# Start-up of a fused S4 and gated-FFN kernel: first factors in two halves, identity on another queue, another order of folds and turns

## The reference

```
xn = layernorm(x)
s  = S4 convolution of xn along the 512 + D * xn      # a 512-tap causal filter
h1 = xn @ w1.T + 2 * (xn @ A1.T) @ B1.T               # 1376 hidden units, rank 16
h3 = xn @ w3.T + 2 * (xn @ A3.T) @ B3.T
y  = (silu(h1) * h3), through w2 with A2, B2 likewise
out = x + s * silu(y)
```

## Time and profile before

| | |
|---|---|
| median of 3 runs | 406.63 us |
| the profiled execution's own time | 406.52 us |
| its span, first to last instruction | 404.7 us |
| TensorE busy | 399.2 us (99%) |
| VectorE, ScalarE, GpSimd busy | 207.4, 111.5, 80.3 us |

### The profile page before, as it was taken

How to read it: one execution, slowest core, us unless ns; L and a number is a source line. 1 busy time by engine, 2 the same in 40 slices (tenths; PEclk the granted TensorE clock), 3 DMA queues, 4 the chain that set the end, 5 groups by cost and what they waited for, 6 DMA issues and landing times.

```text
span 404.7 us, 5106 instructions
## 1 busy us (share of the span) xinstructions
PE 399.2 (99%) x1838; PEld 332.9 (82%) x1838; DVE 207.4 (51%) x323; ACT 111.5 (28%) x185; POOL 80.3 (20%) x141
## 2 busy tenths in 40 slices
PE   8999999999999999999999999999999999999996
PEld 7988888888888888888888888888888888888885
DVE  5877776794883336553345236754236134411227
ACT  7554232222541111222232112222123111211122
POOL 6686745403510113300000101600000000000000
PEclk9999999999999999999999999999999999999999
DMA  8583743614325102000005301000002000000002
GB/s 275 147 218 97 230 149 110 209 41 126 110 89 173 52 2 52 2 1 0 2 1 193 118 0 52 0 0 0 0 0 104 2 0 0 2 0 0 2 0 104
DMA packets 14515, 26.90 MB, mean 66 GB/s; under 512 B 2816, under 2 KB 4576, under 8 KB 14368
## 3 DMA queue, kind: packets, MB, share of 16 engines
q1 hardware_dynamic: 13488, 24.53, 19.1%
q0 software_dynamic: 720, 1.60, 1.5%
q10 hardware_dynamic: 288, 0.52, 0.3%
HBM read 21.45 MB, written 4.54 MB: 64 GB/s over the span
## 4 chain that ended last, share of the span: by engine, by line
PE 95%; DVE 1%; DMA 1%; ACT 1%; issue 1%; POOL 0%; DVEq 0%; ACTq 0%; POOLq 0%
PE h L1173 19%; PE h L1175 19%; PE h L1174 19%; PE f L1173 10%; PE f L1175 10%; PE f L1174 10%; PE h L1196 2%; PE spare L1160 1%; PE spare L1175 1%; PE spare L1173 1%; PE spare L1174 1%; DMA xn<-x_dram 1%; PE spare L1155 1%; DVE xres L946 0%; ACT xn L723 0%
## 5 line engine op out<-in xcount | busy, mean ns | idle before, releaser
L1173 PE MATMUL h<-xt,w 128*128 (+2 forms) x340 | 131.3, 386 | 0.0
L1174 PE MATMUL h<-xt,w 128*128 (+2 forms) x340 | 131.2, 386 | 0.0
L1175 PE MATMUL h<-xt,w 128*128 (+2 forms) x340 | 131.1, 386 | 0.0
L913 DVE TENSOR_TENSOR ghl<-g,ghl 128x512 fp32r<-128x512 f32 x44 | 31.7, 721 | 83.5 <-ACT ghl L715 83.5
L1173 PEld LDWEIGHTS h<-xt,w 128*128 128x128 f32 x340 | 63.9, 188 | 12.8 <-DVE w L852 0.3
L1175 PEld LDWEIGHTS h<-xt,w 128*128 128x128 f32 x340 | 63.9, 188 | 12.8
L1174 PEld LDWEIGHTS h<-xt,w 128*128 128x128 f32 x340 | 63.9, 188 | 12.6
L1173 PE MATMUL f<-ghl,w2f 128*128 128x512 f32 x176 | 68.7, 390 | 0.0
L1174 PE MATMUL f<-ghl,w2f 128*128 128x512 f32 x176 | 68.6, 390 | 0.0
L1175 PE MATMUL f<-ghl,w2f 128*128 128x512 f32 x176 | 68.5, 389 | 0.0
L908 DVE TENSOR_TENSOR g<-g,h 128x512 f32<-128x512 f32 x40 | 27.5, 688 | 77.3 <-PE h L1175 77.2
(11 more groups left out here) (187 smaller groups left out, 353.0 us busy)
## 6 DMA issues: line engine op xcount, KB each, us to landing
raw<-w_dram SPq DMA_DIRECT2D x28, 256.0 KB, 4.0
outT_dram<-xres SPq DMA_DIRECT2D x15, 256.0 KB, 2.4
xres<-xT_dram SPq DMA_DIRECT2D x3, 1024.0 KB, 6.0
rows_next<-x_dram SPq DMA_DIRECT2D x4, 512.0 KB, 3.6
scale_rows<-scales_scratch SPq DMA_DIRECT2D x3, 512.0 KB, 4.1
rows<-x_dram SPq DMA_DIRECT2D x2, 512.0 KB, 6.5
dft_sb<-dft_dram SPq DMA_DIRECT2D x1, 1024.0 KB, 5.0
xres<-xT_dram SPq DMA_DIRECT2D x4, 256.0 KB, 3.9
```

Of the source, the lines that this page charges most:

```text
L913: nc.vector.tensor_tensor(ghl[:, 1, :], g[:, :], ghl[:, 0, :].bitcast(F32), ALU.subtract).then_inc(glo_done, 1)
L1173: pe.matmul(out, w[1], m[0], start=start, stop=False)
L1174: pe.matmul(out, w[0], m[1], start=False, stop=False)
L1175: return pe.matmul(out, w[0], m[0], start=False, stop=stop)
```

## The change

The first factors are stored as two halves, the first for w1, the second for w3. Each half has its own clearing (half on VectorE, half on GpSimd), its own load and semaphore. The identity and the other lane constants are issued on ScalarE's queue behind row tiles 1 and 2. The warm-up has 8 matmuls instead of 11. TensorE does turn 0, fold (1, 1), turn 1, fold (3, 1), and then the first product; the first products of w1 and w3 are taken apart into their three parts, and turns 2 and 3 stand between those. VectorE and ScalarE follow in the order of their work.

```diff
-FIRST_COLS = {1: 2 * D, 3: 2 * D + 2 * P}
+FIRST_COLS = {1: D, 3: 2 * D + 2 * P}
-FACTORS_BY_DVE = 832
+FACTORS = LORA_FIRST // 2
-A_FIRST = {1: 0, 3: D}
+A_FIRST = {1: 0, 3: D + 2 * P}
...
@@ SyncE @@
             load_tile(0)
-            sync.wait_ge(factors_dve, 1)
-            sync.wait_ge(factors_pool, 1)
-            sync.dma_start(lr[0:P:STACK_STEP, :], lora).then_inc(lora_in, 16)
-            sync.dma_start(lane_c[:, :], lanes).then_inc(const_in, 16)
+            for i in range(2):
+                sync.wait_ge(factors_dve, i + 1)
+                sync.wait_ge(factors_pool, i + 1)
+                cols = slice(i * FACTORS, (i + 1) * FACTORS)
+                sync.dma_start(lr[0:P:STACK_STEP, cols], lora[:, cols]).then_inc(lora_in[i], 16)
...
@@ ScalarE @@
             for r in (1, 2):
                 act.dma_start(xn[:, r, :], x[r * P:(r + 1) * P, :]).then_inc(x_in[r], 16)
+            act.dma_start(lane_c[:, :], lanes).then_inc(const_in, 16)
...
             rows_hi(0)
+            rows_hi(1)
             rows_norm(2)
-            rows_hi(1)
             spread_cast(spread_in, slice(0, LANES_EARLY))
+            fold_hi(3, 0)
             rows_norm(3)
-            fold_hi(3, 0)
...
@@ VectorE @@
-            nc.vector.memset(lr[:, 0:FACTORS_BY_DVE], 0.0).then_inc(factors_dve, 1)
+            for i in range(2):
+                nc.vector.memset(lr[:, i * FACTORS:i * FACTORS + FACTORS // 2], 0.0).then_inc(factors_dve, 1)
             rows_first(0)
             rows_first(1)
+            fold_add(1, 0)
             rows_first(2)
-            fold_add(1, 0)
+            fold_add(3, 0)
             rows_first(3)
-            fold_add(3, 0)
             rows_lo(0)
+            rows_lo(1)
             fold_lo(1, 0)
-            rows_lo(1)
...
@@ TensorE @@
+                def part(out, kind, w, m, cols, start, stop):
+                    for c in range(DC):
+                        mm = pe.matmul(out[:, cols], w13_tile(kind, 0, w)[:, c, :], xt[:, 0, m, c, cols],
+                                       start=(start and c == 0), stop=(stop and c == DC - 1))
+                    return mm
...
-                keep_busy(11)
-                pe.wait_ge(lora_in, 16)
+                keep_busy(8)
+                pe.wait_ge(lora_in[0], 16)
                 fold(1, 0)
+                pe.wait_ge(lora_in[1], 16)
                 fold(3, 0)
                 pe.wait_ge(const_in, 16)
                 turn_rows(0)
+                fold(1, 1)
                 turn_rows(1)
-                fold(1, 1)
-                turn_rows(2)
-
+                fold(3, 1)
                 pe.wait_ge(whi_done, 1)
                 pe.wait_ge(xhi_done, RT // 2)
-                for c in range(DC):
-                    pe.matmul(h1[:, lo], w13_tile(1, 0, 0)[:, c, :], xt[:, 0, 0, c, lo], start=(c == 0), stop=False)
-                fold(3, 1)
+                part(h1, 1, 0, 0, lo, True, False)
+                turn_rows(2)
+                pe.wait_ge(xlo_done, RT // 2)
+                part(h1, 1, 0, 1, lo, False, False)
+                wait_split(pe, 1, 0)
+                part(h1, 1, 1, 0, lo, False, True)
                 turn_rows(3)
-                wait_split(pe, 1, 0)
-                pe.wait_ge(xlo_done, RT // 2)
-                for c in range(DC):
-                    pe.matmul(h1[:, lo], w13_tile(1, 0, 1)[:, c, :], xt[:, 0, 0, c, lo], start=False, stop=False)
-                    pe.matmul(h1[:, lo], w13_tile(1, 0, 0)[:, c, :], xt[:, 0, 1, c, lo], start=False, stop=(c == DC - 1))
+                pe.wait_ge(whi_done, 2)
+                part(h3, 3, 0, 0, lo, True, False)
+                part(h3, 3, 0, 1, lo, False, False)
                 wait_split(pe, 3, 0)
-                hidden(0, 0, 0, 3, h3, lo)
+                part(h3, 3, 1, 0, lo, False, True)
+                pe.wait_ge(xhi_done, RT)
+                part(h1, 1, 0, 0, hi, True, False)
+                part(h1, 1, 1, 0, hi, False, False)
                 pe.wait_ge(xlo_done, RT)
-                hidden(0, 0, 0, 1, h1, hi).then_inc(h1_ready, 1)
+                part(h1, 1, 0, 1, hi, False, True).then_inc(h1_ready, 1)
                 hidden(0, 0, 0, 3, h3, hi).then_inc(h3_ready, 1)
...
@@ GpSimd @@
-            nc.gpsimd.memset(lr[:, FACTORS_BY_DVE:LORA_FIRST], 0.0).then_inc(factors_pool, 1)
-            pool.wait_ge(factors_pool, 1)
+            for i in range(2):
+                nc.gpsimd.memset(lr[:, i * FACTORS + FACTORS // 2:(i + 1) * FACTORS], 0.0).then_inc(factors_pool, 1)
+            pool.wait_ge(factors_pool, 2)
...
@@ host @@
-        "lora": _np.concatenate([a1, a3, b1.T[:, :2 * P], b3.T[:, :2 * P]], axis=1),
+        "lora": _np.concatenate([a1, b1.T[:, :2 * P], a3, b3.T[:, :2 * P]], axis=1),
```

More of the change, by code:

```diff
@@ L404, in build @@
         raw_in = [sem(f"raw_in{i}") for i in range(6)]
-        lora_in, const_in = sem("lora_in"), sem("const_in")
+        lora_in, const_in = [sem(f"lora_in{i}") for i in range(2)], sem("const_in")
         spread_in, late_in, stack_cleared = sem("spread_in"), sem("late_in"), sem("stack_cleared")
```

## The result

The changed kernel takes 407.79 us in the median of 12 runs (406.61 to 408.33), the kernel before, beside it, 406.73 us (406.45 to 407.12): a ratio of 1.0023, 95% interval 1.0015 to 1.0031. It is slower by 1.06 us in the medians, where 0.35 us of gain was forecast, and lies outside the range of 405.7 to 407.2. The runs are not one heap: three stand at 406.61 to 406.96, nine at 407.73 to 408.33, and none between. The profiled execution (407.73 us, span 405.9 us) is one of the nine. In a later comparison one run of the changed kernel took 1434 us and two of the kernel before 576 and 1043 us; these three are left out of all that follows.

The account below looks back on a forecast made before the run. After 17.7 us the number of matmuls bounds the kernel, so only hidden tile 1's start counts: TensorE's holes 0.70 for 0.99 us, the rest drains, 17.67 to about 17.3, -0.35 us; 406.3 us predicted, range 405.7 to 407.2.

Parts of the forecast that it names:

- the landing of half 0: First factors' load: issued at about 1.43, taking 3.3 to 3.6 us for 48 KB, landing at 4.7 to 5.0.
- the clock: TensorE's warm-up: eight matmuls end at 4.41, about when the clock rose; rise taken to come as before, price 0.
- add 6.20: VectorE's list: `fold_add(1, 0)` starts at 6.20, in place of the third statistics, once its fold is out.
- rival 2: Half 0 or its weight tile 0.3 to 0.6 us late delays VectorE's list; nothing won, 406.6 to 406.9; chance 0.15.
- the reserve: Margin before a late half 0 or weight tile would delay `fold_add(1, 0)` and all behind it: 0.2 us.
- The weights of that add: Weight load for `fold_add(1, 0)`: goes out behind half 1 at about 2.5 and lands at about 5.6.
- that on `rows_lo(1)`: TensorE, product with the low rows: waits for `rows_lo(1)` until 11.51, a wait of 0.42 us.
- that on `fold_lo(1, 0)`: TensorE, product with the low weights: waits for `fold_lo(1, 0)` until 12.11, 0.12 us more.
- fold (3, 1), whose bank was to be free in time: TensorE after turn 1: bank free at 8.95, fold (3, 1) done by 10.0 without a wait.
- `fold_add(3, 0)` at 8.2: VectorE: second add at 8.19, done 8.9, ahead of the statistics of tile 3.
- rival 3: Clock rises late, from the first fold to the first product: +2.2 us, 408.8 us; chance 0.12.
- the identity's move to ScalarE's queue: ScalarE before its first scaling: issue takes 0.56 of 0.88 us idle, 0.32 us of cover stay, cost 0.

Follow-up runs that it names:

- e7: The changed kernel again, unaltered, with 8 warm-up matmuls, beside the kernel before: 406.89 us in ten runs, ratio 1.0004.
- e4: The changed kernel with 10 warm-up matmuls instead of 8: 407.24 us, ratio 1.0012 to the kernel before.
- e1: The changed kernel with the old 11 warm-up matmuls instead of 8, nothing else: 407.21 us, ratio 1.0012 to the kernel before.
- e3: The changed kernel's new order alone, with factors whole, identity on SyncE's queue and 11 warm-up matmuls as before: 407.25 us, ratio 1.0014 to the kernel before.
- e10: The changed kernel with 11 warm-up matmuls and tile 2's statistics ahead of `fold_add(1, 0)` on VectorE: 406.57 us, ratio 0.9997 to the kernel before.
- e12: The changed kernel a third time, unaltered, with 8 warm-up matmuls, beside the kernel before: 407.85 us, ratio 1.0024.
- e2: The kernel before with 8 warm-up matmuls instead of 11, nothing else: 406.66 us, ratio 1.0005.
- e9: The changed kernel with 4 warm-up matmuls instead of 8: 408.52 us in 6 runs, ratio 1.0048 to the kernel before.
- e6: The kernel before with only the loads changed (factors in halves, identity on ScalarE's queue), old orders and 11 warm-up matmuls: 406.50 us, ratio 0.9993.
- e8: The kernel before with three moves in ScalarE's and TensorE's order, VectorE's list untouched: 406.52 us, ratio 0.9994.

## Why the prediction was wrong

Two steps failed: the landing of half 0, which was mis-sized, and the clock, which was put at nothing. The first costs about 0.1 us in the medians, the second 1.2 us in the runs that it hits, and it alone takes the result out of the range.

**The step that failed first** is the start of VectorE's chain, "add 6.20". It rested on half 0 landing at 4.7 to 5.0. Half 0 landed at 5.0 to 5.5 in the ten traces with halves, 3.5 to 4.0 us after an issue at 1.51, in nine of the ten above the 3.3 to 3.6 that I took, and no row stood behind the 3.3. (The fold was not mis-sized: from its first record to the add behind it pass 1.28 us, e7: 5.37 to 6.65, where 4.8 to 6.20 leaves 1.4.) So the add began at 6.49 to 6.68 where neither clock nor warm-up delayed it, 0.3 to 0.5 us late. That is rival 2 to the letter, and its time, 406.6 to 406.9, is what the early runs have: 406.85, hidden tile 1 at 17.72 and 17.87. I gave it 0.15 and called the reserve 0.2 us; there was none. The weights of that add, which I had landing at 5.6, landed at 5.9 to 6.6, in e4 behind the fold.

**What the forecast had right** is the rest of that chain. It put hidden tile 1 9.1 us after `fold_add(3, 0)`; in e1, e3, e4, e7, e10 and e12, where hidden tile 1 began anywhere from 17.72 to 18.41, it was 9.23 or 9.24. Of the two waits that were to stand in front of the first products, that on `rows_lo(1)` came, at 0.67 us instead of 0.42, and that on `fold_lo(1, 0)` doesn't show. In its place fold (3, 1), whose bank was to be free in time, waited 0.3 to 0.5 us for `fold_add(3, 0)`. In e12 0.33 and 0.67 make 1.00 where the forecast had 0.70 and the kernel before 0.99. With adds at 6.49 to 6.65 and 1.98 us to the second add the sum gives 17.7 to 17.9: the cost of the order where the clock is early is 0.05 to 0.2 us in these traces, 0.1 us in the medians of the early runs. e3, with the loads and the warm-up of before, contradicts that size (0.23 us in its trace, 0.5 us in the medians); the difference stays open.

**A second term was left out.** By putting `fold_add(3, 0)` at 8.2 instead of 9.30, the forecast made the landing of its weights a condition. I took it as given. It was 7.9 in the trace before, and in the ten traces with halves anywhere from 7.8 (e12) to 9.1 (e4), though issued 0.1 us earlier. Past 8.2 it would have held an add that was in time; e4 and e10 waited for it. The old list, whose add comes at 9.3, doesn't.

**The clock, priced at 0,** is the step that made the result. I took the rise "to come as before", from one trace at 4.42, inside the span of eight warm-up matmuls (to 4.49). In the eight traces with 11 it came at 4.42 to 6.68, in seven of them behind 4.49. And 15 of 33 runs of the changed kernel are 1.2 us slower than the other 18 (408.06 to 406.85). This is rival 3, with chance 0.12 and the right place. Its price, 2.2 us, was for a clock that stays low to the first product; in the profile it rose at 9.23, with the two folds and one turn behind it. e1 against the changed kernel, e2 and e9 show that it goes with the length of the warm-up: with 11 matmuls one run of 12 of the changed kernel and one of 107 of the kernel before stand at 407.6 or above, with 8 it is 15 of 33 in the new order and 3 of 11 in the old, with 4 all six. The late rise itself was traced twice (9.23, and 10.17 in e9) and an early one in the three other traces with 8; for the other late runs it is inferred from the time, which isn't sure, since the traced runs of e4 (407.77) and e10 (408.31) had early rises. The Trainium skill's sentence on the rise (page "TensorE: Matmul & The Clock Gate", section "What's actually happening") had been put beside the sum and given no weight in it; the runs agree with it that the point of the rise differs between runs. What stays open is why the share of late runs went from nine of 12 to none of 10 to six of 11 between comparisons of the same kernel; the last two were on different chips.

**Right as well:** the identity's move to ScalarE's queue costs nothing (ScalarE still idled 0.58 us before its first scaling, and began it at 6.44 instead of 6.26 because tile 0's statistics had begun at 4.11 instead of 3.93; in e7 and e12 at 6.37 and 6.28), the loads alone show no cost (e6), and in the changed kernel nothing moved behind hidden tile 1. Nine of the 12 runs are late, so the 1.06 us between the medians are about 0.1 us of order and 1.2 us of clock, less what the median of the twelve, at the low end of the late group, leaves out.

## What to carry to other kernels

An engine's list is served in order: to move an operation forward, ask first when its input is there, and what stands behind it. Here a `fold_add` that was never waited for was moved ahead of two statistics and became the head of the chain that sets the end, together with two loads that had had a microsecond of slack. And a warm-up that ends before its work begins should be timed over many runs before it is cut: here it then ended 0.7 to 0.9 us before that work, the saving (three matmuls that nobody waited for) was nothing, and the price 1.2 us in almost half of the runs. In the same way, a hole closed at the start can open as a wait later (e8): compare the end of the span, not the place of the gain alone.

## What the runs showed of the hardware

- With 11 warm-up matmuls from 1.00 us on, the granted clock rose at 4.42, 4.92, 5.29, 5.54, 5.94, 6.08, 6.31 and 6.68 us in eight profiles; the first of these was the only one that I had. Where the warm-up ends at 4.5, the rise came at 4.77, 5.10, 5.37 and once at 9.23; where it ends at 2.8, at 10.17. The profile's clock column says 1.00 for the stretches ahead of the rise too; the weight loads, 0.33 us at the lower level and 0.19 at the upper, tell it.
- A load of half the size, issued 0.27 us earlier, landed only 0.1 us earlier (3.8 us for 48 KB against 3.6 for 96 KB). Over the traces it is 3.5 to 4.0 us for 48 KB and 3.4 to 3.6 for 96 KB.
- The load of weight tile (3, 0), 256 KB, took 3.8 us (e2) to 5.2 us (e4) from issue to landing.
- Once in a while TensorE pauses near 110 us, at the end of the first block: 0.5 us in the profiles of e3 and e4, and in that of e10 (408.31 us, its median is 406.57) this wait:

```profile
PEld f L1176 <- ACT ghl L716: 1.4, 1, 1.4
```

The other eleven profiles have none. All three have the new order of TensorE, and so have six of the eleven. It is a part of the scatter, and a profile's own time should be read with that in mind. Its cause was not looked for.
